# Weights stored by partition in the inputs of an eight-core retention and mixture-of-experts layer

## The chip, the cores and the metric

The kernel runs on the eight cores of one Trainium2 chip. Each core takes one of the eight sequences of the input (2048 tokens of width 1024) and holds its own copy of all weights; the cores exchange nothing. The metric is device time in microseconds of the slowest core.

## What is computed

One layer in two halves. Everything is given in float32; the kernel multiplies in bfloat16.

```python
x = x + attn(layernorm(x))        # retention, 16 heads of 64
x = x + ffn(layernorm(x))         # 8 experts, 2 per token, and a shared part

# attn: q, k, v per head; scores = (q k^T) * decay; ret = scores v; norm per head
gate = x @ w1                     # 1024 x 1024
out = (silu(gate) + norm) @ w2    # 1024 x 1024

# ffn
probs = softmax(x @ router_w); top 2 of 8 experts
routed = sum over the two of p_e * (silu(x @ w1[e]) @ w2[e])       # 8 x 2 matrices of 1024 x 1024
shared = sigmoid(x @ shared_gate_w) * ((silu(g) * u) @ shared_down) # g, u = halves of x @ shared_gate_up (1024 x 2048)
```

## The kernel before, in words

The weights lie in the inputs as the reference has them, row by row in float32. TensorE wants them in bfloat16 with row k * 128 + p in partition p. DMAs issued by GpSimd (POOL) convert the type on the way, and so all weights pass through the queue that the profile calls q0:

- `cast_rows` (L327) loads a matrix straight into SBUF: `w1a` (L328, the gate), `rout` (the router, nine columns), `w2a`, `wgu` and `wdn` (the shared part). Each partition reads eight rows of the matrix, one for each k, that lie 128 rows apart.
- `cast_step` (L901) converts the experts' matrices from HBM to a bfloat16 copy `wbd` in HBM, in 64 DMAs of 256 source rows each. Each writes two rows of 2 KB side by side in each of 128 partitions.
- `ew_ready` (L974) later loads the converted matrices of an expert into one of four SBUF buffers `ew`, with two DMAs of 2 MB on SP's queue (q1). An expert's partition has 32 KB in `wbd`, and each DMA takes one 16 KB half of it.

The first stage handles the 2048 tokens in eight groups of two tiles (128 tokens each). A program in Python lays the steps of retention, projection, router and shared part of neighbouring groups over one another by due times (the table AT) and emits them in that order to every engine. POOL's order is fixed by it too: it computes the reciprocal roots of the layer norms (L369) and of the head norms (L585), issues the casts of the experts, about nine to a group (L906), and the scatters of the routing table (L820, `metad`). Tiles of x are loaded by SP (`load_x`, L305): tile t + 2 is asked for at the statistics of tile t, tiles 4 and later wait for the first small products since they share their space, and tile t waits for the output of tile t - 10.

SP's order at the start is: x0, wk, x1, four constants, x2, x3, six constants, a block of zeros (`zrow`), the table's padding (`padm`), x4 to x7. ACT issues wq, eye and wv on its own queue (q10). POOL issues `w1a` at once; `rout`, `w2a`, `wgu`, `wdn` come in its program behind the roots of tiles x0 and x1, and the first experts' casts behind those of x4 and x5 (L369).

At the end of the first stage the last four scatters write which token goes where (L820). SP reads the table back (`meta`, L1001), POOL gathers the first expert's tokens with it (L1033), and TensorE transposes them (L1045). Then come the eight experts, first layer L1062, second layer L1106 (L1082 for the last half block), and each block's result is added to the output by an indirect DMA (L1117, L1091). An extra branch for experts with over 576 tokens isn't taken here.

Of the kernel before, what the change touches and what calls it, by code (L numbers as in the profile page):

```python
# [8 lines left out]
BF16 = mybir.dt.bfloat16  # L9
# [5 lines left out]
D = 1024  # L15
T = 2048
NH = 16
NE = 8
# [124 lines left out]
def build():  # L143
    nc = bass.Bass("TRN2", target_bir_lowering=False)
    st = contextlib.ExitStack()

    def din(name, shape, dt=F32):
        return nc.dram_tensor(name, shape, dt, kind="ExternalInput").ap()
# [2 lines left out]
    dwq = din("wqT", [128, NH * 64])  # L151
    dwk = din("wkT", [128, NH * 32])
    dwv = din("wvb", [128, 1024])
    dw1a = din("w1a", [D, D])
    dw2a = din("w2a", [D, D])
    dgns = din("gns", [128, 8])
    dgnb = din("gnb", [128, 8])
    drout = din("rout", [D, 9])
    dwe1 = din("we1", [NE, D, D])
    dwe2 = din("we2", [NE, D, D])  # L160
    dwgu = din("wgu", [D, 2 * D])
    dwdn = din("wdn", [D, D])
    deye = din("eye", [128, 128], BF16)
    dtri = din("tri", [128, 128], BF16)
    dstri = din("stri", [128, 128], BF16)
# [6 lines left out]
    dout = nc.dram_tensor("out", [T + PAD, D], F32, kind="ExternalOutput").ap()  # L172

    dx2r = nc.dram_tensor("x2rd", [T + PAD, D], BF16).ap()
    dwb = nc.dram_tensor("wbd", [NE, 128, 16384], BF16).ap()
    dmeta = nc.dram_tensor("metad", [128 * NSB, 2], I32).ap()
    NPL = EB * NE + 4 * OVC * NE

# [43 lines left out]
    rout = al("rout_sb", [128, 72], BF16)  # L222
# [3 lines left out]
    w1a = al("w1a_sb", [128, 8192], BF16)  # L226
# [14 lines left out]
    w2a = al("w2a_sb", [128, 8192], BF16)  # L241
# [8 lines left out]
    wgu = al("wgu_sb", [128, 16384], BF16)  # L250
    wdn = al("wdn_sb", [128, 8192], BF16)
# [12 lines left out]
    ew = [al(f"ew{i}", [128, 16384], BF16, a) for i, a in enumerate((Z1, Z2, Z3, Z3 + 32768))]  # L264
# [18 lines left out]
    p = Prog(nc, st)  # L283
# [19 lines left out]
    K = {}  # L303
# [21 lines left out]
                       (ones, dones))  # L325

    def cast_rows(dst, src):  # L327
        return lambda e: e.dma_start(out=dst[:, :].rearrange("p (k f) -> p k f", k=8),  # L328
                                     in_=src.rearrange("(k p) f -> p k f", p=128))
    k_w1a = p.dma("gpsimd", s_w["w1a"], cast_rows(w1a, dw1a[:, :]))  # L330

    k_z = [p.op("vector", lambda e, i=i: e.memset(sbd[i][:, :], 0.0)) for i in range(2)]
# [568 lines left out]
    def cast_step(e_, w_, q):  # L901
        src = (dwe1, dwe2)[w_]

        def f():
            a = 8192 * w_ + 2048 * q
            k_cast[e_] = p.dma("gpsimd", s_cast[e_], lambda e: e.dma_start(  # L906
                out=dwb[e_, :, a:a + 2048].rearrange("p (k f) -> p k f", k=2),
                in_=src[e_, 256 * q:256 * q + 256, :].rearrange("(k p) f -> p k f", p=128)))
        return f
    casts = [cast_step(e_, w_, q) for e_ in range(NE) for w_ in range(2) for q in range(4)]  # L910

# [1 line left out]
    for f in (a0, b0, score_weights, c0, a1, b1, c1_, center):  # L913
# [5 lines left out]
        out=dx2r[T:T + PAD, :].rearrange("(b p) f -> p b f", p=128),  # L919
        in_=zrow[:, :].unsqueeze(1).broadcast_to([128, PAD // 128, D])), k_pre0)  # L920
# [53 lines left out]
    def ew_ready(e_, *ws):  # L974
        for w_ in range(2):
            k_ew[e_, w_] = p.dma("sync", s_ew[2 * e_ + w_], lambda e, w_=w_: e.dma_start(
                out=ew[e_ % 4][:, 8192 * w_:8192 * w_ + 8192], in_=dwb[e_, :, 8192 * w_:8192 * w_ + 8192]),
                k_cast[e_], *ws)
    ew_ready(0, end_1)


# [17 lines left out]
    for f in sct7:  # L999
        f()  # L1000
    k_meta = p.dma("sync", s_meta, lambda e: e.dma_start(  # L1001
        out=meta[:, :].rearrange("p (b c) -> p b c", c=2), in_=metad[:, 0:EB * NE, :]), K["sct"])
    k_meta4 = None
    for h in range(2):
        k_meta4 = p.dma("sync", s_meta4, lambda e, h=h: e.dma_start(
            out=meta4[64 * h:64 * h + 64, :].rearrange("p (b c) -> p b c", c=2),
            in_=metad[0:64, 0:EB * NE, :]), K["sct"], end_1)
# [3 lines left out]
    k = p.op("vector", lambda e: e.tensor_reduce(flag[:, :], carry[:, :], AXX, ALU.max), vecf)  # L1011
# [138 lines left out]
    for eng in ("tensor", "vector", "scalar"):  # L1150
# [4 lines left out]
        out=ovm[:, :].rearrange("p (b c) -> p b c", c=2), in_=metad[:, EB * NE:NPL, :]), k_acc)  # L1155
    ovf = ovm[:, :].bitcast(F32)
    last = None
    for e_ in range(NE):
        for w_, src in enumerate((dwe1, dwe2)):
            kw = p.dma("gpsimd", s_ovw, lambda e, e_=e_, w_=w_, src=src: e.dma_start(  # L1160
                out=ew[0][:, 8192 * w_:8192 * w_ + 8192].rearrange("p (k f) -> p k f", k=8),
                in_=src[e_, :, :].rearrange("(k p) f -> p k f", p=128)), last, K["L2", NE - 1])
        for c in range(OVC):
            n0 = 4 * (OVC * e_ + c)
            kf = []
            for i in range(4):
                n = n0 + i
                kx = p.dma("gpsimd", s_xs[i], lambda e, n=n, i=i: e.indirect_dma_start(
                    out=xs[i][:, :], out_offset=None, in_=dx2r[:, :],
                    in_offset=bass.IndirectOffsetOnAxis(ap=ovm[:, 2 * n:2 * n + 1], axis=0)), last, k_om)  # L1170
                kb, bank, w = rot.take()
                bv = as_bf(bank)

                def fl(e, i=i, bv=bv):
                    for q in range(8):
                        m = e.transpose(bv[:, 128 * q:128 * q + 128], xs[i][:, 128 * q:128 * q + 128],
                                        eye[:, :])
                    return m
                k = p.op("tensor", fl, kx, w)
                kf.append(p.op("vector", lambda e, i=i, bv=bv: e.tensor_copy(  # L1180
                    xst[0][:, 0:4096].rearrange("p (k s) -> p k s", k=8)[:, :, 128 * i:128 * i + 128],
                    bv.rearrange("p (k s) -> p k s", k=8)), k, K.get("ovl1")))
                rot.done(kb, kf[-1])
            kh = []
            for f_ in range(8):
                kb, bank, w = rot.take()

                def f1(e, f_=f_, bank=bank):
                    for q in range(8):
                        m = e.matmul(bank[:, :], ew[0][:, 1024 * q + 128 * f_:1024 * q + 128 * f_ + 128],  # L1190
                                     xst[0][:, 512 * q:512 * q + 512], start=(q == 0), stop=(q == 7))
                    return m
                K["ovl1"] = k = p.op("tensor", f1, kf, kw, w)
                kh.append(p.op("scalar", lambda e, f_=f_, bank=bank: e.activation(
                    hT[0][:, 512 * f_:512 * f_ + 512], bank[:, :], AF.Silu), k, K.get("ovl2")))
                rot.done(kb, kh[-1])
            done = []
            for i in range(4):
                n = n0 + i
                ky = []  # L1200
                for h in range(2):
                    kb, bank, w = rot.take()

                    def f2(e, i=i, h=h, bank=bank):
                        for q in range(8):
                            m = e.matmul(bank[:, :], hT[0][:, 512 * q + 128 * i:512 * q + 128 * i + 128],
                                         ew[0][:, 8192 + 1024 * q + 512 * h:8192 + 1024 * q + 512 * h + 512],
                                         start=(q == 0), stop=(q == 7))
                        return m
                    K["ovl2"] = k = p.op("tensor", f2, kh, w)  # L1210
                    ky.append(p.op("scalar", lambda e, i=i, h=h, n=n, bank=bank: e.mul(
                        yb[i][:, 512 * h:512 * h + 512], bank[:, :], ovf[:, 2 * n + 1:2 * n + 2]), k,
                        k_acc, last, k_om))
                    rot.done(kb, ky[-1])
                done.append(p.dma("gpsimd", s_acc[i], lambda e, i=i, n=n: e.indirect_dma_start(
                    out=dout[:, :], out_offset=bass.IndirectOffsetOnAxis(ap=ovm[:, 2 * n:2 * n + 1], axis=0),
                    in_=yb[i][:, :], in_offset=None, compute_op=ALU.add), ky, done))
            last = [done, K["ovl1"], K["ovl2"]]
# [21 lines left out]
def _host_prep(inputs):  # L1240
    gam = _gammas()
    bf = lambda x: np.ascontiguousarray(x).astype(ml_dtypes.bfloat16)
    f32 = lambda x: np.ascontiguousarray(x, dtype=np.float32)
# [18 lines left out]
    p = np.arange(128)  # L1262
    vtab = np.zeros((128, NT, NH))
    for t in range(NT):
# [6 lines left out]
    rcon[:, 0:16] = np.tile(8.0 - e8, 2)[None, :]  # L1271
    rcon[:, 16:32] = np.tile(128 * EB * e8, 2)[None, :]
    rcon[:, 32:48] = np.tile(128 * EB * NE - CAP + (512 * OVC - 128 * EB) * e8, 2)[None, :]
    rout = np.concatenate([np.asarray(inputs["L0_ffn_router_w"]),
                           np.asarray(inputs["L0_ffn_shared_gate_w"])], axis=1)
    return {
        "wqT": f32(wqT.reshape(128, -1)), "wkT": f32(wkT.reshape(128, -1)),
        "wvb": f32(wvb.reshape(128, -1)),
        "w1a": f32(inputs["L0_attn_w1"]), "w2a": f32(inputs["L0_attn_w2"]),
        "gns": f32(np.asarray(inputs["L0_attn_gn_scale"]).reshape(8, 128).T),  # L1280
        "gnb": f32(np.asarray(inputs["L0_attn_gn_bias"]).reshape(8, 128).T),
        "rout": f32(rout),
        "we1": f32(inputs["L0_ffn_w1"]), "we2": f32(inputs["L0_ffn_w2"]),
        "wgu": f32(inputs["L0_ffn_shared_gate_up"]), "wdn": f32(inputs["L0_ffn_shared_down"]),
        "eye": bf(np.eye(128)), "tri": bf(tri), "stri": bf(stri), "ones": bf(np.ones((128, 128))),
        "sel": bf(sel), "selb": bf(selb.reshape(16, -1)),
        "vtab": f32(vtab.reshape(128, -1)), "etab": f32(etab.reshape(128, -1)),
# [17 lines left out]
```

How the kernel before makes its waits and increments, by code:

```python
        def go(e):  # L85
            for sem, value in need:
                e.wait_ge(sem, value)
            return fn(e)
# [2 lines left out]
    def op(self, eng, fn, *ws):  # L91
        sem = self.eng_sem[eng]
        self.count[eng] += 1
        self.raw(eng, lambda e: fn(e).then_inc(sem, 1), *ws)
        return Tok(sem, self.count[eng])
# [4 lines left out]
    def dma(self, eng, sem, fn, *ws):  # L100
        total = self.dma_total.get(sem.name, 0) + 16
        self.dma_total[sem.name] = total
        self.raw(eng, lambda e: fn(e).then_inc(sem, 16), *ws)
        return Tok(sem, total)
```

## Time and profile before

| | us |
|---|---|
| median of 3 runs | 814.59 (810.98 to 815.88) |
| the profiled execution | 814.13 |
| its span, slowest core | 812.6 (cores from 807.7 to 812.6) |
| first stage, to TensorE's last product before the routed tokens | 479.4 |
| TensorE begins on the experts | 517.4 |

The span is what lies between a core's first and last instruction; the profiled execution's time is 1.5 us longer. All numbers of the trace are of core 7, the slowest, unless a core is named. Its DMA queues are q0 (POOL), q1 (SP) and q10 (ACT). A DMA is cut into packets, and the 16 DMA engines take a share of the packets each; the profile gives bytes as they are written, so that a float32 matrix that arrives as bfloat16 counts half of what is read.

### The profile page before, as it was taken

The page shows a single profiled execution, that of the slowest core. Times are in us where ns is not written, and L with a number is a line of the kernel's source. Part 1 is how long each engine was busy: PE and PEld are TensorE (multiplying, and loading weights), DVE is VectorE, ACT ScalarE, POOL GpSimd, SP SyncE. Part 2 cuts the span into 40 slices and gives each one's busy share as a digit, 9 for nine tenths or more (in the row PEclk, how much of TensorE's full clock was granted, in tenths as well). Part 3 has the DMA queues.
Part 4 walks back from the last instruction along what each step waited for, and adds up shares of the span by engine and source line. Part 5 has one row for each costly group of instructions (what it writes and reads, how often), then busy time and mean ns, then how long its engine had stood idle before and what let it go on. Part 6 is the DMA issues. An engine that isn't in the chain of part 4 may idle for free.

```text
span 812.6 us, 15482 instructions; the slowest of 8 cores (807.7 to 812.6 us)
## 1 busy us (share of the span) xinstructions
PE 676.5 (83%) x5736; PEld 453.4 (56%) x5736; DVE 322.9 (40%) x872; ACT 282.6 (35%) x482; POOL 247.0 (30%) x241
## 2 busy tenths in 40 slices
PE   2478799797997997988987850499999999999990
PEld 2354585574764855756665630376575765756650
DVE  4446577486584773854857620110010100101000
ACT  2363633434426334343142100033333343333430
POOL 1242504414226044133240300424344243440321
PEclk9978999899898998998999985599999999999996
DMA  9999999999999999999999994869999998992843
GB/s 193 218 206 153 180 134 114 149 150 111 126 149 138 135 131 134 111 110 149 108 128 250 146 235 50 262 227 171 242 231 199 266 208 219 237 218 41 117 57 64
DMA packets 44640, 131.30 MB, mean 162 GB/s; under 512 B 7040, under 2 KB 7424, under 8 KB 42512
## 3 DMA queue, kind: packets, MB, share of 16 engines
q0 software_dynamic: 32336, 72.41, 67.3%
q1 hardware_dynamic: 11792, 56.75, 24.9%
q10 hardware_dynamic: 432, 1.08, 0.5%
q8 instruction: 49, 0.80, 0.4%
q14 instruction: 31, 0.25, 0.1%
HBM read 141.35 MB, written 66.49 MB: 256 GB/s over the span
## 4 chain that ended last, share of the span: by engine, by line
PE 66%; DVE 11%; DMA 9%; issue 5%; POOL 3%; ACT 2%; another core or an unknown queue 1%; SPq 1%; DVEq 0%; POOLq 0%; ACTq 0%
PE P L1062 16%; PE P L1106 14%; PE P L843 13%; DMA metad<-ext,pos 5%; PE P L458 4%; PE P L654 4%; DMA xr<-x 3%; DVE stt L364 3%; PE P L868 2%; PE P L1045 2%; POOL rstd L585 2%; DVE pb L507 2%; PE P L1082 2%; PE P L442 1%; PE P L416 1%
## 5 line engine op out<-in xcount | busy, mean ns | idle before, releaser
L1062 PE MATMUL P<-xst,ew 128*128 128x288 bf16 x1024 | 134.9, 289 | 1.1 <-DVE xst L1049 1.1
L843 PE MATMUL P<-x2T,wgu_sb 128*128 128x256 bf16 x1024 | 129.7, 291 | 0.5 <-DVE xr L879 0.5
L843 PEld LDWEIGHTS P<-x2T,wgu_sb 128*128 128x128 bf16 x1024 | 105.8, 105 | 20.1 <-issue 1.0
L1062 PEld LDWEIGHTS P<-xst,ew 128*128 128x128 bf16 x1024 | 98.6, 99 | 28.7 <-issue 4.2
L1106 PE MATMUL P<-ew,hT 128*128 128x512 bf16 x512 | 111.8, 379 | 0.0
L1049 DVE COPY xst<-P 128x1024 bf16<-128x1024 bf16 (+1 forms) x40 | 25.5, 638 | 209.3 <-PE P L1045 209.3
L1069 ACT ACTIVATE hT<-P 128x288 bf16<-128x288 f32 x128 | 52.7, 412 | 141.5 <-PE P L1062 81.9
L585 POOL TENSOR_TENSOR rstd<-gtmp,mhalf 128x16 bf16<-128x16 f32 x16 | 46.7, 2918 | 175.4 <-DVE gtmp L581 175.4
L1117 POOL DMA_INDIRECT out<-yb,meta x32 | 50.4, 1575 | 107.9 <-ACT yb L1112 84.0
L1106 PEld LDWEIGHTS P<-ew,hT 128*128 128x128 bf16 x512 | 50.0, 98 | 58.9
L1033 POOL DMA_INDIRECT xs<-x2rd,meta x40 | 38.1, 952 | 117.0 <-PE P L1045 63.0
L1112 ACT ACTIVATE yb<-P,meta 128x512 f32<-128x512 f32 x64 | 44.1, 689 | 69.1 <-PE P L1106 65.9
L654 PE MATMUL P<-w2a_sb,gate 128*128 128x512 bf16 x256 | 61.3, 384 | 5.9 <-DVE gtmp L581 3.3
L868 PE MATMUL P<-wdn_sb,sgu 128*128 128x512 bf16 x256 | 60.5, 379 | 5.1 <-issue 4.1
L458 PE MATMUL P<-xnt,w1a_sb 128*128 128x256 bf16 x512 | 64.2, 281 | 0.0
L1045 PE MATMUL P<-eye_sb,xs 128*128 128x128 bf16 (+1 forms) x320 | 24.2, 222 | 38.6 <-DMA xs<-x2rd,meta 38.6
L458 PEld LDWEIGHTS P<-xnt,w1a_sb 128*128 128x128 bf16 x512 | 49.5, 100 | 11.0 <-issue 2.1
L369 POOL TENSOR_TENSOR mv<-mv,mhalf 128x1 f32<-128x1 f32 x32 | 17.8, 555 | 114.1 <-DVE mv L368 111.0
L672 ACT ACTIVATE x<-xr,mv 128x1024 bf16<-128x1024 f32 x16 | 19.9, 1244 | 81.4 <-DVE mv L374 81.2
L364 DVE BATCH_NORM_STATS2 stt<-xr 128x6 f32<-128x512 f32 x64 | 41.0, 683 | 13.0 <-DMA xr<-x 12.7
L906 POOL DMA_DIRECT2D wbd<-we x64 | 45.3, 720 | 0.0
L1045 PEld LDWEIGHTS P<-eye_sb,xs 128*128 128x128 bf16 (+1 forms) x320 | 20.5, 101 | 42.8 <-issue 41.2
(134 smaller groups left out, 834.2 us busy)
## 6 DMA issues: line engine op xcount, KB each, us to landing
wbd<-we POOLq DMA_DIRECT2D x64, 512.0 KB
ew<-wbd SPq DMA_DIRECT2D x16, 2048.0 KB, 23.3
xr<-x SPq DMA_DIRECT2D x16, 512.0 KB, 16.4
out<-xr SPq DMA_DIRECT2D x16, 512.0 KB, 17.5
wgu_sb<-wgu POOLq DMA_DIRECT2D x1, 4096.0 KB, 61.4
x2rd<-x SPq DMA_DIRECT2D x16, 256.0 KB
w1a_sb<-w1a POOLq DMA_DIRECT2D x1, 2048.0 KB, 29.2
w2a_sb<-w2a POOLq DMA_DIRECT2D x1, 2048.0 KB, 35.3
```

Source lines behind the costliest of these rows:

```text
L364: a = [p.op("vector", lambda e, h=h: e.bn_stats(sv[:, 6 * h:6 * h + 6], src[:, 512 * h:512 * h + 512]), k_src, K.get(("mvfree", i))) for h ...
L458: last = e.matmul(bank[:, GT * j:GT * j + GT], w1a[:, 1024 * k + 128 * mm:1024 * k + 128 * mm + 128], xv[:, GT * k:GT * k + GT], start=(k ...
L585: K["rs", t] = p.op("gpsimd", lambda e: e.tensor_tensor(rstd[:, 32 * par + 16 * i:32 * par + 16 * i + 16], gtmp[:, 16 * i:16 * i + 16], mh ...
L654: last = e.matmul(bank[:, :], gate[par][:, GT * k + 128 * i:GT * k + 128 * i + 128], w2a[:, 1024 * k + 512 * h:1024 * k + 512 * h + 512], ...
L843: last = e.matmul(bank[:, GT * j:GT * j + GT], wgu[:, 2048 * k + a:2048 * k + a + 128], x2T[b][:, GT * k:GT * k + GT], start=(k == 0), sto ...
L868: last = e.matmul(bank[:, :], sgu[:, GT * k + 128 * i:GT * k + 128 * i + 128], wdn[:, 1024 * k + 512 * h:1024 * k + 512 * h + 512], start= ...
L906: k_cast[e_] = p.dma("gpsimd", s_cast[e_], lambda e: e.dma_start(out=dwb[e_, :, a:a + 2048].rearrange("p (k f) -> p k f", k=2), in_=src[e_ ...
L1045: last = e.transpose(bv[:, n * k:n * k + n], xs[i][0:n, 128 * k:128 * k + 128], eye[0:n, 0:n])
L1062: last = e.matmul(bank[:, 0:HC], ew[e_ % 4][:, 1024 * k + 128 * f_:1024 * k + 128 * f_ + 128], xst[e_ % 2][:, CAP * k + HC * c:CAP * k + H ...
L1069: K["h", e_, c] = p.op("scalar", lambda e: e.activation(hT[e_ % 2][:, CAP * f_ + HC * c:CAP * f_ + HC * c + HC], bank[:, 0:HC], AF.Silu), ...
L1106: last = e.matmul(bank[:, :], hT[e_ % 2][:, CAP * k + 128 * i:CAP * k + 128 * i + 128], ew[e_ % 4][:, 8192 + 1024 * k + 512 * h:8192 + 102 ...
L1117: K["acc", n] = p.dma("gpsimd", s_acc[n % 4], lambda e: e.indirect_dma_start(out=dout[:, :], out_offset=bass.IndirectOffsetOnAxis(ap=meta[ ...
```

## The change

Each weight matrix comes in as 128 rows, one for each partition, with the eight pieces of the partition side by side. The function `rows` on the host makes that order. Loads and casts then take whole rows: 32 KB of float32 that become 16 KB of bfloat16 (64 KB and 32 KB for `wgu`, 288 bytes for the router). A cast of an expert's matrix, of which there are still four to a matrix, now takes 32 whole partitions, every fourth one, and each matrix of `wbd` is one contiguous block of 2 MB. The number of DMAs, their order, their waits and their bytes are as before.

```diff
-    dw1a = din("w1a", [D, D])
-    dw2a = din("w2a", [D, D])
+    dw1a = din("w1a", [128, 8192])
+    dw2a = din("w2a", [128, 8192])
-    drout = din("rout", [D, 9])
-    dwe1 = din("we1", [NE, D, D])
-    dwe2 = din("we2", [NE, D, D])
-    dwgu = din("wgu", [D, 2 * D])
-    dwdn = din("wdn", [D, D])
+    drout = din("rout", [128, 72])
+    dwe1 = din("we1", [NE, 128, 8192])
+    dwe2 = din("we2", [NE, 128, 8192])
+    dwgu = din("wgu", [128, 16384])
+    dwdn = din("wdn", [128, 8192])
-    dwb = nc.dram_tensor("wbd", [NE, 128, 16384], BF16).ap()
+    dwb = nc.dram_tensor("wbd", [NE, 2, 128, 8192], BF16).ap()
     def cast_rows(dst, src):
-        return lambda e: e.dma_start(out=dst[:, :].rearrange("p (k f) -> p k f", k=8),
-                                     in_=src.rearrange("(k p) f -> p k f", p=128))
+        return lambda e: e.dma_start(out=dst[:, :], in_=src)
...
         def f():
-            a = 8192 * w_ + 2048 * q
             k_cast[e_] = p.dma("gpsimd", s_cast[e_], lambda e: e.dma_start(
-                out=dwb[e_, :, a:a + 2048].rearrange("p (k f) -> p k f", k=2),
-                in_=src[e_, 256 * q:256 * q + 256, :].rearrange("(k p) f -> p k f", p=128)))
+                out=dwb[e_, w_, q:128:4, :], in_=src[e_, q:128:4, :]))
...
             k_ew[e_, w_] = p.dma("sync", s_ew[2 * e_ + w_], lambda e, w_=w_: e.dma_start(
-                out=ew[e_ % 4][:, 8192 * w_:8192 * w_ + 8192], in_=dwb[e_, :, 8192 * w_:8192 * w_ + 8192]),
+                out=ew[e_ % 4][:, 8192 * w_:8192 * w_ + 8192], in_=dwb[e_, w_, :, :]),
                 k_cast[e_], *ws)
...
+    rows = lambda w: f32(np.asarray(w).reshape(*np.shape(w)[:-2], 8, 128, -1).swapaxes(-3, -2).reshape(
+        *np.shape(w)[:-2], 128, -1))
```

## Rows read from the trace of the kernel before

**Rows 1.** The page: busy shares, the span in 40 slices, POOL's queue.

```profile
PE 676.5 (83%) x5736; PEld 453.4 (56%) x5736; DVE 322.9 (40%) x872; ACT 282.6 (35%) x482; POOL 247.0 (30%) x241
PEclk9978999899898998998999985599999999999996
DMA  9999999999999999999999994869999998992843
GB/s 193 218 206 153 180 134 114 149 150 111 126 149 138 135 131 134 111 110 149 108 128 250 146 235 50 262 227 171 242 231 199 266 208 219 237 218 41 117 57 64
...
q0 software_dynamic: 32336, 72.41, 67.3%
```

**Rows 2.** The timeline of TensorE from 472 us: start, length, line [idle before, releaser].

```profile
472.35 7.07 PE L868 MATMUL P<-wdn_sb,sgu 128*128 128x512 bf16 x32 [1.01 <-DVE sgu L854]
517.41 1.01 PE L1045 MATMUL P<-eye_sb,xs 128*128 128x128 bf16 x8 [37.99 <-DMA xs<-x2rd,meta]
```

**Rows 3.** The chain that ended last, in order of time: start, length, what.

```profile
466.07 40.08 DMA metad<-ext,pos
506.22 1.88 DMA meta<-metad
...
509.26 1.00 POOL xs L1033
510.53 8.25 DMA xs<-x2rd,meta
```

**Rows 4.** The same chain of core 4.

```profile
456.92 45.26 DMA metad<-ext,pos
```

**Rows 5.** The stretches of one group and one expert: busy us by engine, PEclk, DMA share, GB/s.

```profile
205.00:260.00 55.00, 50.25 (x471) 34.49 (x470) 35.87 (x102) 22.82 (x38) 18.76 (x21) 0.93 1.05 140
...
658.00:692.00 34.00, 34.00 (x252) 21.67 (x252) 3.19 (x5) 12.80 (x25) 12.65 (x10) 1.00 0.92 221
```

**Rows 6.** DMA queues, 18 to 24 us: packets, MB, share of 16 engines.

```profile
q0 software_dynamic: 382, 0.78, 80.2%
q1 hardware_dynamic: 387, 0.51, 29.3%
```

**Rows 7.** DMA queues, 42 to 48 us.

```profile
q0 software_dynamic: 226, 0.46, 58.7%
q1 hardware_dynamic: 227, 0.80, 43.2%
```

**Rows 8.** DMA queues, 60 to 70 us.

```profile
q0 software_dynamic: 350, 1.43, 99.0%
```

**Rows 9.** DMA queues, 120 to 135 us.

```profile
q0 software_dynamic: 844, 1.63, 99.9%
```

**Rows 10.** DMA queues, 471 to 476 us.

```profile
q1 hardware_dynamic: 80, 1.23, 79.0%
q0 software_dynamic: 89, 0.16, 22.9%
```

**Rows 11.** DMA queue of SP, 0 to 60 us, and 24 to 30 us.

```profile
q1 hardware_dynamic: 3424, 6.33, 37.7%
...
q1 hardware_dynamic: 768, 0.81, 52.1%
```

**Rows 12.** The timeline of POOL: start, length, line [idle before, releaser].

```profile
16.95 0.55 POOL L369 TENSOR_TENSOR mv<-mv,mhalf 128x1 f32<-128x1 f32 x1 [5.85 <-DVE mv L368]
...
23.14 0.89 POOL L328 DMA_DIRECT2D w2a_sb<-w2a  x1
...
57.20 0.55 POOL L369 TENSOR_TENSOR mv<-mv,mhalf 128x1 f32<-128x1 f32 x1
57.70 4.16 POOL L906 DMA_DIRECT2D wbd<-we  x6
...
466.07 0.96 POOL L820 DMA_INDIRECT metad<-ext,pos  x1 [0.27 <-issue]
```

**Rows 13.** Who waited for x: us in total, times, longest; SP's issue; x loads' landing.

```profile
DVE stt L364 <- DMA xr<-x: 12.7, 4, 4.1
...
28.14 2.17 SPq L306 DMA_DIRECT2D xr<-x  x4
...
xr<-x SPq DMA_DIRECT2D x16, 512.0 KB, 16.4
```

More of the change, by code:

```diff
@@ L1160, in build @@
             kw = p.dma("gpsimd", s_ovw, lambda e, e_=e_, w_=w_, src=src: e.dma_start(
-                out=ew[0][:, 8192 * w_:8192 * w_ + 8192].rearrange("p (k f) -> p k f", k=8),
-                in_=src[e_, :, :].rearrange("(k p) f -> p k f", p=128)), last, K["L2", NE - 1])
+                out=ew[0][:, 8192 * w_:8192 * w_ + 8192], in_=src[e_, :, :]), last, K["L2", NE - 1])
         for c in range(OVC):
@@ L1278, in _host_prep @@
         "wvb": f32(wvb.reshape(128, -1)),
-        "w1a": f32(inputs["L0_attn_w1"]), "w2a": f32(inputs["L0_attn_w2"]),
+        "w1a": rows(inputs["L0_attn_w1"]), "w2a": rows(inputs["L0_attn_w2"]),
         "gns": f32(np.asarray(inputs["L0_attn_gn_scale"]).reshape(8, 128).T),
         "gnb": f32(np.asarray(inputs["L0_attn_gn_bias"]).reshape(8, 128).T),
-        "rout": f32(rout),
-        "we1": f32(inputs["L0_ffn_w1"]), "we2": f32(inputs["L0_ffn_w2"]),
-        "wgu": f32(inputs["L0_ffn_shared_gate_up"]), "wdn": f32(inputs["L0_ffn_shared_down"]),
+        "rout": rows(rout),
+        "we1": rows(inputs["L0_ffn_w1"]), "we2": rows(inputs["L0_ffn_w2"]),
+        "wgu": rows(inputs["L0_ffn_shared_gate_up"]), "wdn": rows(inputs["L0_ffn_shared_down"]),
         "eye": bf(np.eye(128)), "tri": bf(tri), "stri": bf(stri), "ones": bf(np.ones((128, 128))),
```

## The prediction

> **What bounds the kernel now.** First the page. TensorE is busy for 83% of the span, but the DMA engines stand at nine tenths from the second slice to the twenty-fifth, while they write only 110 to 150 GB/s over most of it [rows 1]. The stretches show two regimes [rows 5]. In a group of the first stage (55 us) TensorE works for 50 us and the DMA share is above 1; in an expert (34 us) TensorE is busy for the whole 34.0 us, and DMAs there cost nothing. So the question is the first stage.
>
> TensorE's timeline shows one hole: its last product of the first stage ends at 479.42, the next begins at 517.41, 38 us later, and what ends the wait is the gather of the first tokens [rows 2]. The chain says what the gather waited for [rows 3]: the last scatter of the routing table, issued at 466.07 on POOL, takes 40.08 us to land, for 8 bytes a row. The table's load (1.88 us), POOL and the gather (8.25 us) follow. The scatter is a small thing at the end of a long queue: casts go through q0 too, and they were behind. Core 4 tells the same: its scatter left 9 us earlier, at 456.92, and landed at 502.2, hardly earlier [rows 4]. The end of the first stage is set by when the DMA engines are through with their work, not by when the scatter is asked for.
>
> **The price of a cast.** A packet's time is the share times 16 engines times the stretch, over the packets. Into SBUF, 2 KB written (4 KB read) takes 0.802 x 96 / 382 = 0.201 us [rows 6]; `wgu`, with runs twice as long, 0.990 x 160 / 350 = 0.453 us for 4 KB written, or 0.226 us for 2 KB [rows 8]. So a run of double length was no cheaper by the byte. From HBM to HBM, a 2 KB packet takes 0.999 x 240 / 844 = 0.284 us [rows 9]. The trace has no HBM to HBM packet over 2 KB, so what the change makes of 0.284 us isn't shown. Its bounds are 0.201 us (only the destination's place costs, the nearest row below) and 0.32 us for 2 KB (0.284 worsened as `wgu` is against rows 6, by 12%). A cast moves three bytes through HBM for each it writes: 1.63 MB in 15 us is 326 GB/s of HBM traffic, and the `wgu` load's 1.43 MB in 10 us is 286 GB/s of reading. Both are of the size of the best stretches, in which large loads of plain type land 1.23 MB in 5 us, 246 GB/s, beside casts of 0.16 MB (another 96 GB/s through HBM) [rows 10]. That looks like memory with eight cores on it, not like a cost by the packet, and I take 0.284 us as it is: no gain from longer runs.
>
> The Trainium skill, HBM Reference, Specifications, gives about 358 GB/s for each core of a pair; by that figure the cast-only stretch has 9% left at most, an estimate of some 26 us over the 291 us that all casts cost. It also puts the size needed for line rate at 512 bytes (DMA: Bandwidth & Descriptors, Specifications), and by that rule the runs were long enough before; the rows agree between 2 and 4 KB.
>
> **What a turn is.** An engine takes packets from its queues in turns. From 42 to 48 us q0 moved 226 packets and q1 227 [rows 7], from 18 to 24 us 382 and 387 [rows 6]. From 471 to 476 us q1's packets are 16 KB rows of `ew` (1.23 MB in 80), q0's 2 KB, and it is still 89 to 80 [rows 10]: one for one whatever the size, and q1 has 79% of the engines' time then. So whoever has the longer rows gets the engine. The change gives q0 rows of 16 KB, with 8 x 0.226 = 1.8 us each into SBUF and 8 x 0.284 = 2.3 us in HBM. That each row stays one packet is a reading: q1's 16 KB rows are one each, and `wgu`'s 4 KB too (350 packets, 1.43 MB). The other end is that q0's packets stay at 4 KB, the longest that this queue shows.
>
> The Trainium skill has the turns too (DMA: Bandwidth & Descriptors, Queues, rings and completion order): an engine goes round its queues and drains one packet, typically 9 to 17 descriptors, from each. Were q0's turn already nine 2 KB rows, it would last 2.6 us before as after, the start below would lose nothing, and the sum would stay near 814 us. The trace's one for one speaks against that reading.
>
> **The start.** This is where small packets of x now meet long ones of the weights. SP's order up to x7 is 3,424 packets by 60 us [rows 11], and x4 to x7 are the last 512 of them. Before x5 is complete, 3,168 must be through, 198 for each engine. x4 and x5 matter since POOL issues the first casts behind the root of x5 at 57.20 [rows 12], and TensorE's second group needs both tiles. Step by step with rows of 16 KB:
> - `w1a` starts at about 8.5 us as before. Its 8 rows for each engine take turns with one packet of q1 and one of q10 each, about 2.1 us a turn: done at 25 us. q1 is then near 384 packets, which is x0, wk and x1. x1 is at hand at about 26 us rather than before the root at 16.95.
> - `w2a` is 6.2 us behind that root in POOL's program [rows 12]. It leaves at about 34 us and moves at 38. In between q1 is almost alone: at 768 packets in 6 us [rows 11] it would finish, but SP issues `zrow`, `padm` and x4 to x7 (28.14 before [rows 13]) also some 10 us later. I put q1 at 2,300 of 3,168 by 38 us, so 54 are left for each engine. x2 and x3 come by 36 us rather than 30, six lost.
> - Now `w2a`, `wgu` and `wdn`: 256 pieces of 2 KB for each engine, between 0.201 and 0.226 us, so 51 to 58 us; I take 55. They are 24 rows (32 if `wgu`'s are cut in two), and q1 gets 24 packets in between (5 us); the other 30 cost 6 us. x5 is there at 38 + 55 + 5 + 6 = 104 us instead of 57: **+47 us**, and TensorE and POOL stand still for it. If q0's packets stay at 4 KB, a turn is 0.2 us longer over some 50 turns: +10 us. The upper end is +55.
>
> **The later groups.** Nine casts a group are 146 pieces for each engine, 42 us, and q1's 48 packets (two loads, two outputs, two `x2rd`) another 10: 52 of 54.5 us. The order shifts, the work fits. But a load of x waits for an output to land, and both now take turns of 2.3 + 0.2 us against a median of 16.4 us to landing [rows 13]: eight packets are 20 us. Today only the first four tiles are waited for, 12.7 us in total [rows 13]. I take +4 us for three such loads, from 0 to 12.
>
> **The hand-over.** What TensorE loses at the start, the casts make up: they wait for x5 themselves, so the loads of the weights are through before the first is issued, and the backlog of about 42 us that stood through the first stage isn't built. So the last scatter, at 466.07 + 47, doesn't wait 40.08 us. It still has 16 rows of `ew` for each engine beside it (0.790 x 80 / 80 = 0.79 us each [rows 10], 13 us at most); bounds are 3 us and 13 us, I take 6. That is **-34 us**. The clock comes back after that hole in any case (two slices at 0.5 [rows 1]); it now has a hole at the start too, for about 1 us.
>
> **At nothing.** `rout` becomes 128 packets rather than 1,024, some 4 us of q0 that the start's sum already holds. Issues on POOL cost about 0.7 us a cast [rows 12] with idle time around. The contiguous `ew` loads lie beside TensorE in the experts; without that cover they would decide, but 34.0 of 34 us are TensorE's [rows 5].
>
> **Sum**, against the profiled execution's 814.13 us (its span and 1.5 us around it, and 0.5 us under the median of 814.59): 814.13 + 47 + 4 - 34 + 1 = **832 us**.
>
> **Rivals.**
> 1. *The casts do get cheaper and the turns don't hurt* (cheaper runs in HBM, or an engine that cuts long rows so that x passes). For it: 0.284 against 0.201 us for the same 2 KB is a difference of place that may be one of runs. Against it: `wgu`. From 0.25 us downwards the 1,024 pieces for each engine are 35 us less and the backlog is gone. Then the scatter takes 3 us, and the rest of the chain (3.1 us to POOL's gather, 8.2 to TensorE) ends at 467 + 3 + 11.3 = 481 us, just behind TensorE's own end. That is 36 us gained, about 5 lost to the loads of `ew`: **784 us**, between 775 and 800.
> 2. *Nothing but the router's load changes*: packets are cut to the old size, or to 4 KB with +10 us at the start that the queue's end gives back. The work of the engines is what it was, less 4 us: **811 us**, 805 to 818.
> 3. *Slower, and further than I say*: SP's queue starves in every group. The place is the six casts that POOL issues in a row at the start of a group: 12 rows of 2.3 us for each engine. An output and the load that waits for it can then take 20 us each, one behind the other, and the load is asked for about 22 us before its tile is due. From a landing of about 25 us on, each of four groups loses 10 us or more: **860 us**.
>
> **How the numbers follow.** Forecast 0.50, rival 1 0.27, rival 2 0.15, rival 3 0.08. The forecast's own range is 816 (lower ends of start and groups) to 848 (both upper ends and the scatter at 13). The range for all must reach into rival 1: 782 to 848 leaves out rival 3 and the fastest part of rival 1, under 0.2. A measurement here tells no change from one within about 1%, 806.4 to 822.7 us. Slower is four fifths of the forecast and rival 3, 0.48; the rest of the forecast and most of rival 2 is the same, 0.22; rival 1 and a little of rival 2 is faster, 0.30.
>
> **What would show it.** q0's packets fall from 32,336 [rows 1] to about half (the gathers, scatters and results stay), and rows of 16 KB appear; if they don't, rival 2 holds or the weaker start. x5's root stands near 100 us, with TensorE idle before it for over 30 us: the start. The last scatter lands in under 13 us: the hand-over. TensorE's group keeps about 55 us, or rival 3. The price of 2 KB in a cast-only stretch stays near 0.284 us, or rival 1. I am wrong if long rows don't hold an engine for their whole length, and wrong by the other sign if they do but cost much less.

## The result, and the profile after

| | before | after |
|---|---|---|
| median, us | 814.69 (810.98 to 815.88, 4 runs) | 835.08 (832.13 to 835.27, 4 runs) |
| span of the profiled execution, slowest core | 812.6 | 833.6 |
| spans of all its cores | 807.7 to 812.6 | 805.3 to 833.6 |

The ratio is 1.0249, between 1.0216 and 1.0283: 20 us slower, where 832 us had been forecast. After the change core 4 is the slowest, and the rows of after are core 4's. Its own span before was 810.0 us. Some executions run slower, with the cores of one die at a lower clock: all ratios leave them out, the medians in us hold every run, and E2's profiled execution is read on its other die, cores 4 to 7.

The page of after, with the share of the DMA engines in 40 slices and the two large queues (packets, MB, share of 16 engines over the span):

```profile
span 833.6 us, 15437 instructions; the slowest of 8 cores (805.3 to 833.6 us)
PE 676.8 (81%) x5691; PEld 455.1 (55%) x5736; DVE 322.9 (39%) x872; ACT 281.0 (34%) x482; POOL 233.6 (28%) x241
DMA  8899999999999999989797947797999999992743
q0 software_dynamic: 13520, 72.41, 61.2%
q1 hardware_dynamic: 11792, 56.75, 25.7%
```

TensorE has the same work as in [rows 1]. POOL's queue carries the same 72.41 MB in 13,520 packets instead of 32,336, and its share fell: 0.612 x 833.6 = 510 us of the engines' time, where core 7 had 0.673 x 812.6 = 547 us before. Compared core by core, the DMA engines had 21 to 38 us less to do (34 us on core 4; 27 us on core 0, from 67.8% of 810.5 to 64.5% of 809.9), and the kernel is 20 us slower all the same. The slices say how: inside the first stage, slices 18, 20, 22 and 24 stand at 8, 7, 7 and 4 where [rows 1] have 9. The engines wait in the middle of the stage that they used to bound.

**The turns.** DMA queues of after, each a stretch named here: 40 to 50 us (rows of `w2a`, 16 KB as written), then 60 to 80 us (rows of `wgu`, 32 KB), then 130 to 140 us (casts beside x):

```profile
q0 software_dynamic: 83, 1.36, 99.9%
q1 hardware_dynamic: 84, 0.27, 8.7%
...
q0 software_dynamic: 102, 3.34, 95.6%
q1 hardware_dynamic: 102, 0.39, 6.9%
...
q0 software_dynamic: 98, 1.08, 98.5%
q1 hardware_dynamic: 95, 0.16, 4.7%
```

In [rows 6, 7] the two queues shared packet for packet with 2 KB rows; they still do, with rows of 16 and 32 KB, each of them one packet (3.34 MB in 102). SP's queue gets 8.7% and 6.9% of the engines in these stretches, where it had 43.2% and 29.3% in those of [rows 7, 6]. The Trainium skill (DMA: Bandwidth & Descriptors, Queues, rings and completion order) lets a turn hold 9 to 17 descriptors; these counts show turns of one row, whatever its length.

**The start.** POOL's timeline (start, length, line): the root of x1, the issue of `w2a`, the root of x5 with the first casts behind it, the last cast, the last scatter:

```profile
27.04 0.55 POOL L368 TENSOR_TENSOR mv<-mv,mhalf 128x1 f32<-128x1 f32 x1 [16.30 <-DVE mv L367]
33.23 0.55 POOL L328 DMA_DIRECT2D w2a_sb<-w2a  x1
87.48 0.55 POOL L368 TENSOR_TENSOR mv<-mv,mhalf 128x1 f32<-128x1 f32 x1 [20.59 <-DVE mv L373]
87.98 3.04 POOL L904 DMA_DIRECT2D wbd<-we  x6
465.51 0.57 POOL L904 DMA_DIRECT2D wbd<-we  x1
519.40 0.96 POOL L819 DMA_INDIRECT metad<-ext,pos  x1 [0.31 <-issue]
```

The same on core 4 before: first casts 57.08, last cast 408.76, last scatter 456.92. So the first casts are 30.9 us late, the last one 56.8, the scatter 62.5.

**The middle.** Who waited for x (us in total, times, longest), and from the chain that ended last, in order of time (start, length, what):

```profile
DVE stt L363 <- DMA xr<-x: 73.3, 7, 22.0
```

```profile
33.53 27.78 DMA xr<-x
...
206.18 38.88 DMA out<-xr
245.13 5.58 DMA xr<-x
...
293.25 20.18 DMA out<-xr
...
354.23 8.25 DMA xr<-x
...
519.40 8.35 DMA metad<-ext,pos
527.82 1.99 DMA meta<-metad
...
532.26 7.09 DMA xs<-x2rd,meta
```

Before it was 12.7 us of waiting, all of it in the first four tiles [rows 13]. Now there are seven waits of up to 22 us, and the chain names the cause of those in the middle: an output takes 38.9 us to land, and SP asks for the next tile of x only then, since both use one buffer. SP's own timeline shows it standing still between the two, and a load of x issued just ahead of the output:

```profile
205.76 0.33 SPq L306 DMA_DIRECT2D xr<-x  x1
206.18 0.38 SPq L883 DMA_DIRECT2D out<-xr  x1
245.13 0.33 SPq L306 DMA_DIRECT2D xr<-x  x1
```

The DMA queues between 206.2 and 245 us:

```profile
q0 software_dynamic: 367, 3.85, 90.9%
q1 hardware_dynamic: 288, 1.05, 10.2%
```

So 18 packets for each engine went through SP's queue in 39 us: eight rows of the load, eight of the output behind them, and two more. At 38.8 / 18 = 2.2 us a turn that is the whole 38.9 us. The pair of a load and an output 0.4 us behind it comes again at 313.49 and 313.91 us, and SP's next load leaves at 354.23. The output of 293.25 is no comparison for it: only 1.56 MB of q0's went beside it, and it landed in 20.18 us.

**The hand-over.** The last scatter lands in 8.35 us instead of 40.08 and 45.26 us [rows 3, 4]. TensorE's first work on the experts:

```profile
536.65 0.99 PE L1042 MATMUL P<-eye_sb,xs 128*128 128x128 bf16 x8 [3.44 <-issue]
```

That is 17.25 us behind the scatter's issue, where core 4 had 55.6 us before (456.92 to 512.50). From there to the end it is 297.0 us, and was 297.5.

### The profile page after: what moved, and what is told of

Its sections match the earlier page's. It is cut to its first block, busy times and chain, and to the rows that moved or that the text cites. A ratio compares the mean times of both kernels' runs of the same rounds, so it can differ in the third digit from the quotient of the medians.

```text
span 833.6 us, 15437 instructions; the slowest of 8 cores (805.3 to 833.6 us)
## 1 busy us (share of the span) xinstructions
PE 676.8 (81%) x5691; PEld 455.1 (55%) x5736; DVE 322.9 (39%) x872; ACT 281.0 (34%) x482; POOL 233.6 (28%) x241
## 3 DMA queue, kind: packets, MB, share of 16 engines
q0 software_dynamic: 13520, 72.41, 61.2%
## 4 chain that ended last, share of the span: by engine, by line
PE 51%; DMA 17%; DVE 12%; issue 10%; another core or an unknown queue 3%; POOL 2%; ACT 2%; DVEq 1%; SPq 0%; ACTq 0%; POOLq 0%
PE P L1059 15%; PE P L1103 13%; PE P L842 8%; DMA xr<-x 8%; DMA out<-xr 7%; PE P L653 3%; DVE stt L363 2%; PE P L457 2%; PE P L1042 2%; DVE u L638 2%; PE P L1079 2%; DVE gate L642 2%; DVE pb L506 1%; POOL rstd L584 1%
## 5 line engine op out<-in xcount | busy, mean ns | idle before, releaser
L842 PE MATMUL P<-x2T,wgu_sb 128*128 128x256 bf16 x1024 | 132.2, 294 | 1.1 <-issue 0.6
L1103 PE MATMUL P<-ew,hT 128*128 128x512 bf16 x496 | 109.7, 379 | 0.9 <-ACT hT L1066 0.2
L867 PE MATMUL P<-wdn_sb,sgu 128*128 128x512 bf16 x237 | 57.5, 379 | 2.8 <-DVE sgu L853 1.2
L404 ACT ACTIVATE xn<-xr,mv 128x1024 bf16<-128x1024 f32 x16 | 19.8, 1237 | 77.4 <-DVE mv L373 77.4
L653 PEld LDWEIGHTS P<-w2a_sb,gate 128*128 128x128 bf16 x256 | 23.9, 100 | 33.6 <-issue 10.3
L506 DVE TENSOR_TENSOR pb<-P,tri_sb 128x512 bf16<-128x512 f32 x64 | 41.0, 683 | 2.7 <-PE P L497 2.4
## 6 DMA issues: line engine op xcount, KB each, us to landing
out<-xr SPq DMA_DIRECT2D x16, 512.0 KB, 10.3
```

The lines of the kernel that those rows point to most:

```text
L506: kk.append(p.op("vector", lambda e, n=n, b=b: e.tensor_tensor(dst[:, 512 * n:512 * n + 512].rearrange("p (s f) -> p s f", s=4), b[:, :].r ...
L653: last = e.matmul(bank[:, :], gate[par][:, GT * k + 128 * i:GT * k + 128 * i + 128], w2a[:, 1024 * k + 512 * h:1024 * k + 512 * h + 512], ...
L842: last = e.matmul(bank[:, GT * j:GT * j + GT], wgu[:, 2048 * k + a:2048 * k + a + 128], x2T[b][:, GT * k:GT * k + GT], start=(k == 0), sto ...
L867: last = e.matmul(bank[:, :], sgu[:, GT * k + 128 * i:GT * k + 128 * i + 128], wdn[:, 1024 * k + 512 * h:1024 * k + 512 * h + 512], start= ...
L1103: last = e.matmul(bank[:, :], hT[e_ % 2][:, CAP * k + 128 * i:CAP * k + 128 * i + 128], ew[e_ % 4][:, 8192 + 1024 * k + 512 * h:8192 + 102 ...
```

## The experiments

The experiments used three chips, and the kernel before ran at 815.88, 829.5 and 828.87 us on them; so times are compared on one chip only, and each ratio is to the kernel before on its chip. "x5's root", "the last scatter" and the like are medians over the eight cores of a profiled execution, from POOL's timeline: 55.5 and 455.5 us before, 87.2 and 509.9 us after.

### Which rows: all short, or the loads' or the casts' long

The first four keep the changed kernel's layout, with the router's load long, and cut its rows by 64 floats of padding behind each piece. E1 cuts everything to the old length, E2 only the casts, E3 only the loads, E4 everything to 2,048 elements. The core of E1, beside the changed kernel:

```diff
-    dwe1 = din("we1", [NE, 128, 8192])
+    dwe1 = din("we1", [NE, 128, 8704])
...
+    def cut(src, n):
...
+        return src.rearrange("p (k g) -> p k g", g=n + 64)[:, :, 0:n]
...
-                out=dwb[e_, w_, q:128:4, :], in_=src[e_, q:128:4, :]))
+                out=fit(dwb[e_, w_, q:128:4, :], 1024), in_=cut(src[e_, q:128:4, :], 1024)))
```

> The changed kernel with its new layout in memory, but each row cut into the old pieces: 4 KB read and 2 KB written (8 KB and 4 KB for wgu), by 256 bytes of padding between pieces in the inputs. Only the router's load stays long. Theory of turns (long packets on POOL's queue hold each engine and starve SP's queue): the loss is gone, x5's root is back near 57 us, the last scatter again waits about 40 us, 808 to 815 us against 814.6 before and 835 after. Rival, layout (the places and strides in HBM cost, not the packets): still 830 to 838 us. If short pieces with long contiguous reads are cheaper in memory: under 805 us.

> Long rows only for w1a, w2a, wgu, wdn and the router; the experts' casts are cut to 2 KB written. Theory of turns: the start keeps its loss (x5's root near 87 us rather than 57), the groups then go without a wait for x, and with the backlog gone the last scatter lands in under 10 us: 30 lost and about 32 given back, 810 to 819 us. Rival, layout: 825 us or more if the loads' layout costs, 814 with x5's root near 57 us if it doesn't. If the loss sat in the casts alone: the start at 57 us.

> Long rows only for the experts' casts (16 KB written, 2.3 us of an engine each); the loads of w1a, w2a, wgu, wdn are cut to the old pieces. Theory of turns: x5's root stays near 57 us, then SP's queue starves in the groups: waits for x of 20 us and more after outputs that take 30 us and more to land, 35 to 60 us up to the last scatter, and 30 of them given back at the hand-over: 820 to 840 us. Rival, only the start matters: x5's root at 57 us and no later waits, 805 to 815 us.

> All weights in pieces of 8 KB read and 4 KB written. Theory of turns: a turn of q0 is 0.45 to 0.57 us, x5's root 5 to 12 us later than 57, hardly a wait for x in the groups, the scatter's wait shorter by what the start lost, 808 to 816 us. Also the missing row, a cast of 4 KB from HBM to HBM: 0.57 us a packet if it goes by bytes; 0.45 us or less would be a gain from longer runs and give 795 us or less.

| | us | ratio | x5's root | waits for x | last scatter |
|---|---|---|---|---|---|
| E1, all short | 824.14 | 1.0082 [1.0051, 1.0114] | 70.8 | 30.7 | 468.0 |
| E2, loads long | 827.58 | 1.0112 [1.0060, 1.0164] | 86.7 | 46.6 | 479.1 |
| E3, casts long | 827.10 | 1.0151 [1.0099, 1.0203] | 71.0 | 72.7 | 509.6 |
| E4, 4 KB pieces | 816.62 | 1.0014 [0.9982, 1.0046] | 84.8 | 44.8 | 483.7 |

The two halves of the change act where the prediction had them. Long loads set x5's root: 86.7 us in E2 and 87.2 in the changed kernel, 71 in E1 and E3. Long casts set the waits for x in the later groups. The totals of the table mix these with the start, so here are the waits behind 95 us alone, medians over the eight cores: 28 us in the changed kernel, 41 in E3, and none in E1, E2 and E4 or in the kernel before. The slowest core's waits in E3, of which 41.0 us lie behind 95 us:

```profile
DVE stt L372 <- DMA xr<-x: 71.8, 10, 14.3
```

Several expectations failed. With all rows short, but the router's long, x5 was still at 70.8 us and not near 57, and E1 wasn't back at the time of before; E6 and E12 take that up. In E2 the last scatter was to land in under 10 us, and on cores 4 and 7 it took 32.18 and 35.72 us: with short casts the engines' work still ends the stage, however late it starts. E4's x5 was to be 5 to 12 us later and came 29 us later, half of which the router explains (E1, E6). It has 45 us of waits for x, nearly all at the start, and a scatter that leaves 28 us later than before, and still no loss that can be measured: TensorE is at the experts at 512.6 us (median), where it was at 513.6 before. The shorter backlog behind the last scatter gives back all of it.

### The amount of work: eight casts fewer

E5 is the kernel before without the casts of the second matrices of experts 1 and 3, which use their neighbour's instead, so its result is another one.

```diff
+            if w_ == 1 and e_ in (1, 3):
+                return
```

> The kernel before without 8 of its 64 casts (the second matrices of experts 1 and 3 aren't converted; those experts use the second matrix of the expert before them), so 4 MB less written by casts, 36 us of each engine's time at 0.284 us for 2 KB. If the 38 to 50 us hole before the experts is the engines' backlog, it shrinks by about 33 us and the time is 778 to 788 us. If it is the scatter's own latency or an order of queues, it stays and so does 814 us.

794.20 us, 0.9562 [0.9534, 0.9590]: 36 us less for eight casts of 64, whose pieces are 128 for each engine. That is 36 us at the 0.284 us of [rows 9], but 40 us at the median price of before and 43 us at E5's own (below). So most of the work's price comes back, and the exact agreement with 0.284 us is chance. TensorE's timeline of E5 (core 0), its last product of the first stage and the first on the experts:

```profile
464.74 7.07 PE L868 MATMUL P<-wdn_sb,sgu 128*128 128x512 bf16 x32 [1.01 <-DVE sgu L854]
497.83 1.01 PE L1047 MATMUL P<-eye_sb,xs 128*128 128x128 bf16 x8 [26.02 <-DMA xs<-x2rd,meta]
```

There is still a hole of 26 us (8 to 30 us over the cores; 38 to 51 in the profile of the kernel before). So before the change the engines' work does bound the stage, and rival 1's 36 us for some 35 us less work was sound as a price.

### The router's small packets

E6 is the kernel before with the router's load alone in 128 packets.

```diff
-    drout = din("rout", [D, 9])
+    drout = din("rout", [128, 72])
...
-    k_rout = p.dma("gpsimd", s_w["rout"], cast_rows(rout, drout[:, :]))
+    k_rout = p.dma("gpsimd", s_w["rout"], lambda e: e.dma_start(out=rout[:, :], in_=drout[:, :]))
```

> The kernel before with nothing changed but the router's load: 128 packets of 288 bytes read rather than 1,024 of 36 bytes. In the first experiment (all old pieces, router long) x5's root came at 70 us, not 57. Theory: the router's many tiny packets on POOL's queue were cheap turns, in which SP's queue moved one packet each at the start; without them those packets pair with 2 KB pieces of w2a. Then x5's root is at 65 to 72 us here too, and the time 812 to 820 us. Rival: that delay came from the padded pieces or the new places; then x5's root stays at 57 us and the time is 809 to 815 us.

837.44 us, 1.0068 [1.0027, 1.0110], and x5's root at 72.6 us. DMA queues from 24 to 36 us, first E6 (core 3), then the kernel before (core 7):

```profile
q0 software_dynamic: 812, 1.35, 76.9%
q1 hardware_dynamic: 826, 0.90, 28.9%
```

```profile
q1 hardware_dynamic: 1448, 1.82, 59.9%
q0 software_dynamic: 1447, 0.82, 58.1%
```

One for one in both. But before, about 1,000 of q0's turns were the router's rows of 36 bytes, which took little of q0's time (its share is 58.1% with them and 76.9% without) and let 622 more packets of SP's queue through. A load that looks wasteful was what let x through. It also accounts for E1, whose other rows are all short: 1.0082 there, 1.0068 here, with intervals that overlap. Beside it the long loads (E2, 1.0112) and the long casts (E3, 1.0151) cost about 0.4% and 0.8%, the first no more than the intervals leave open, and all of it together 2.5%, somewhat more than the parts.

### x first, and outputs from another queue

E7 is the changed kernel with x4 to x7 asked for ahead of `zrow` and `padm`. E8 does that too, and stores the outputs from ACT's queue some steps later, so that SP never waits for them.

```diff
+    for t in range(4, 8):
+        load_x(t)
```

```diff
-                K["out", t] = p.dma("sync", s_out[t % NX], lambda e: e.dma_start(
+                def go(t=t, x=x):
+                    K["out", t] = p.dma("scalar", s_out[t % NX], lambda e: e.dma_start(
...
+                late.append(go)
```

> The changed kernel with x4 to x7 asked for ahead of the block of zeros and the table's padding on SP's queue. Theory of turns: x5's root returns to 50 to 60 us, so the start's 30 us are back; then the casts pile up behind the loads as before and SP's queue starves in the groups for longer: waits for x in the groups 50 us or more, last scatter at 500 us or later, 815 to 835 us. Rival, the start was all that was lost: 800 to 806 us.

> As the run with x4 to x7 ahead, and the output tiles of the first stage stored from ACT's queue a few steps later, so that outputs and loads of x no longer stand behind one another in one queue and each queue has its own turn. Theory of turns: the waits for x in the groups fall below 20 us in all, and the cheaper bytes of the long rows are then kept: 785 to 808 us. If the order within SP's queue is not what makes x late, it is like the run without it.

E7: 844.67 us, 1.0198 [1.0146, 1.0250]. x5's root is at 61.8 us, 25 us earlier than in the changed kernel, and the loss is nearly the same. The edit did a second thing, though: `zrow` and `padm` now stood behind x4 to x7 and came among the long rows. On core 4 `padm` took 105.9 us to land, and 8.8 us in the changed kernel:

```profile
metad<-padm SPq DMA_DIRECT2D x1, 136.0 KB, 105.9
```

```profile
ACT x2T L689 <- DMA metad<-padm: 47.4, 1, 47.4
```

In the program ACT's first copy of `x2T` waits for both (`K["gu", -2]`). ACT stood still for 42.8 to 48.5 us on all eight cores, and TensorE with it, 48.3 us on core 4. Behind that the chain of core 4 goes on:

```profile
192.74 13.91 DMA out<-xr
207.13 40.07 DMA out<-xr
247.27 18.16 DMA xr<-x
...
329.81 39.66 DMA out<-xr
369.56 14.60 DMA xr<-x
```

Outputs take 40 us here too (both were issued 0.4 us behind a load of x), SP waits for them, and the last scatter leaves at 520.6 us, no earlier than in the changed kernel. But the waits for x behind 95 us are 14 us (median), less than the changed kernel's 28. What used up the 25 us is first of all the wait for `padm`, which is longer than they are. So E7 doesn't show what an early x5 alone would bring, and it doesn't decide between its two expectations.

E8: four runs of 838.32, 844.25, 877.64 and 911.63 us, too far apart for a ratio; the lowest two are 1.1% and 1.8% over the kernel before. Its profiled execution, the fastest of them, has 26.8 us of waiting for x, of which 8 us behind 95 us, and still the last scatter at 517 us. It has the same wait for `padm`, 43.2 to 48.4 us over its cores, so what the other queue alone is worth stays open.

### Long rows where they can do least harm

E9 is the kernel before with long rows for the casts of experts 5 to 7 only, the last 24; E10 for those of experts 4 to 7; E11 is E9 with long loads of the weights and the router and x4 to x7 first. E12 has the changed kernel's layout of the experts' matrices and of `wbd`, but each cast takes every second partition and every second piece, so that its packets keep the old length.

```diff
+            if e_ >= LONG:
+                k_cast[e_] = p.dma("gpsimd", s_cast[e_], lambda e: e.dma_start(
+                    out=dwb[e_, q:128:4, 8192 * w_:8192 * w_ + 8192],
+                    in_=(dwl1, dwl2)[w_][e_ - LONG, q:128:4, :]))
+                return
```

```diff
+            def part(x):
+                return x[q % 2:128:2, :].rearrange("p (k c f) -> p k c f", c=2, f=1024)[:, :, q // 2, :]
...
+                out=part(dwb[e_, w_]), in_=part(src[e_])))
```

> The kernel before, with long rows only for the casts of experts 5 to 7, the last 24 of 64: they are issued after about 280 us, when nearly all tiles of x have been asked for, so that a starved SP queue can no longer make x late. If long rows cost an engine 0.293 us for 2 KB in such stretches rather than 0.322, 24 casts save 11 us of each engine's work, and as the first stage ends with that work the time is 6 to 13 us under before. If the turns still hurt there (x15, outputs, ew): no gain or a loss of up to 5 us.

> The same with experts 4 to 7, 32 casts, from about 245 us on: 15 us of work saved, but x13 to x15 are still to be asked for. Theory of turns: waits for x of 5 to 20 us come back in one or two groups, which the backlog covers in part: 5 to 15 us under before. If late tiles of x cost in full, slower than the run with three experts.

> The casts of experts 5 to 7 long, those of 0 to 4 as before, the loads of w1a, w2a, wgu, wdn and the router long, and x4 to x7 asked for ahead of the zeros and the padding. The start costs what the run with x4 to x7 ahead showed, x5's root at 62 us rather than 57; the loads' cheaper bytes and the router save 12 us of the engines' work and the late casts 11: 12 to 23 us under before. If the start's 5 us and the later x1 cost in full on top of an unchanged end: 0 to 8 us under.

> The kernel before with the experts' matrices and wbd laid out by partition as in the change, but each cast takes every second partition and every second piece, so that all packets stay at 4 KB read and 2 KB written, without padding; router and loads as before. The run with short padded pieces cost 0.342 us for 2 KB in cast-only stretches against 0.322 before. If the places cost that, it is 0.335 us or more here and the time 8 to 16 us over before; if it was the padding or the router, 0.322 us and no change within 4 us.

| | us | ratio | x5's root | waits for x | last scatter |
|---|---|---|---|---|---|
| E9, experts 5 to 7 | 827.50 | 0.9982 [0.9951, 1.0013] | 56.6 | 17.0 | 480.4 |
| E10, experts 4 to 7 | 829.79 | 1.0019 [0.9985, 1.0053] | 56.6 | 24.1 | 487.1 |
| E11, mixed | 831.95 | 1.0044 [1.0014, 1.0074] | 61.7 | 18.6 | 502.1 |
| E12, new places, short | 828.06 | 0.9987 [0.9952, 1.0021] | 56.4 | 13.6 | 454.9 |

E12's slowest core waits for x as the kernel before did:

```profile
DVE stt L364 <- DMA xr<-x: 13.7, 4, 4.7
```

E12 settles where the loss of the casts lies: with the experts' matrices laid out by partition and the packets short, nothing is lost and nothing gained. For the other weights E1 beside E6 says the same within their intervals. It is the length of the packets, not the places in memory. The price of E12's casts, which was to tell too, doesn't decide: as a mean over the stretches of the next section it is 0.340 us, the size expected if the places cost (0.322 before, 0.342 in E1), as a median 0.320 (0.315 and 0.322). E9 spared most loads of x, and the starving moved to what SP's queue carries at the stage's end. ACT waited for `x2rd` to land, 12.9 to 24.9 us over its eight cores, and not at all in E12. Core 5's wait, and its chain:

```profile
ACT x L675 <- DMA x2rd<-x: 24.9, 2, 18.2
```

```profile
463.67 42.57 DMA x2rd<-x
507.25 17.33 DMA meta<-metad
```

Its last scatter leaves 25 us later than E12's (medians). E10 and E11 didn't gain what was expected of them either; E11 takes E7's order over, and with it a wait for `padm` of 8.5 to 19.5 us. No version beat the kernel before.

### What a cast costs, over all kernels

From all 10 us stretches of cores 0, 2, 4 and 7 (4 to 7 in E2) between 110 and 470 us in which q1 has under 1.5% of the engines: q0's share of the 160 us, over its bytes in pieces of 2 KB, median, in us.

| chip | casts short | casts long |
|---|---|---|
| before and after, profiled | 0.315 | 0.297 |
| first (E1, E2; E3) | 0.322, 0.319 | 0.296 |
| second (E5, E6; E7, E8) | 0.336, 0.317 | 0.298, 0.301 |
| third (E12) | 0.320 | |

E4's pieces of twice the old length cost 0.315. Within each line long rows are 5 to 11% cheaper. At 0.297 us a core moves 16 x 3 x 2,048 bytes in that time, an estimate of 331 GB/s of HBM traffic. The Trainium skill (HBM Reference, Specifications) has 358 GB/s for a core; the runs stay under it, and long rows come nearer.

## Why the prediction was right, and where its terms were off

The time (832 against 835.08) and the mechanism hold; two terms were wrong, the start by 16 us and the groups by 28 us, with opposite signs. Core 4's own sum, from its rows above: +30.9 (start) + 25.8 (from the first cast to the last, 351.7 us before and 377.5 after) + 5.7 (last cast to last scatter, 48.2 and 53.9) - 38.3 (scatter to TensorE) - 0.5 (the rest) = 23.6 us, which is its 833.6 against 810.0.

- **What a turn is** held in full: one row for one row, at 16 and at 32 KB, and rows stay whole. q0's packets are less than half (13,520 of 32,336). Rival 2, that nothing but the router changes, falls with it.
- **The start: +47 predicted, 30.9 measured.** The steps up to `w2a` came as written (x1's root 27.04 against 26, `w2a` 33.23 against 34). The failing step is "I put q1 at 2,300 of 3,168 by 38 us". From 0 to 40 us it was:

```profile
q1 hardware_dynamic: 2827, 4.22, 38.9%
```

  So only 341 packets, 21 for each engine, were left, and they found their turns beside the loads. The 54 of the prediction had SP issuing `zrow`, `padm` and x4 to x7 some 10 us late; x4 to x7 left at 33.53 us against 28.14 [rows 13], and almost alone on the engines q1 went 500 packets further. From 24 to 36 us:

```profile
q1 hardware_dynamic: 2085, 2.44, 62.8%
...
q0 software_dynamic: 145, 0.02, 2.7%
```

  `wgu` was cheaper too: 0.956 x 320 us over 1,631 pieces (3.34 MB) is 0.188 us for 2 KB, against 0.226 us before [rows 8].
- **`rout` at nothing** was wrong in kind. It was costed by the 4 us of q0's engines that it frees; what it gave was turns. E6 shows 16 us at x5's root (72.6 against 56.7 in E5 on the same chip) and 0.7% of the time for this line alone. No run shows the 4 us. In the prediction's sum it is part of the start, which came out smaller all the same.
- **The groups: +4 predicted, 25.8 and 5.7 measured on core 4.** The step that failed is "I take +4 us for three such loads". The landing of an output was put at eight turns, 20 us. The one at 293.25 took as long, with fewer long rows beside it; the one at 206.18 took 38.9 us, and 40.07 and 39.66 stand on E7's chain. The turns were sized about right, 2.2 us by the stretch from 206.2 to 245 us against 2.5. What was left out is that the output stands behind the rows of the load of x that SP issues 0.4 us before it, 18 turns instead of eight. The waits for x behind 95 us came to 26 us on core 4. That is rival 3's place (an output, and the load that waits for it): where it has 10 us or more lost in each of four groups, core 4 lost 31 in all. The cores differ a lot in this (spans of 805.3 to 833.6 us; from first to last cast the medians are 350.8 and 374.3 us, 23.5 lost), and why it hits some more than others is open.
- **The hand-over: -34 predicted, -38.3 measured.** The reason given holds: the backlog isn't built when the casts wait, and the scatter lands in 8.35 us where 6 was taken.
- **No gain from longer runs** was wrong by 6%: 0.315 to 0.297 us in stretches of casts alone, 18 us of the engines' work over 1,024 pieces (21 to 38 us for all of q0, from the pages of the eight cores). The 0.284 us of [rows 9] came from a favourable stretch, and `wgu`'s, on which the choice leaned, compared 4 KB with 2 KB and nothing longer. It changed the end little, since the engines now stand idle in the middle; E9 to E11 try to take that gain without the loss and give 0.998 to 1.004. E5 shows what less work is worth where x keeps pace. So rival 1's saving was about half real (18 us of its 35), and its second condition, that the turns don't hurt, is what failed.

In the sum: 47 + 4 - 34 + 1 = 18 us predicted over the span, 23.6 measured on core 4. The closeness of the number is luck, as the start was 16 us too dear and the groups 28 too cheap. The mechanism isn't: one cause, the long row's turn, stands behind both terms, and E2 has the first without the second, E3 the second without the long loads. Whether an earlier x5 would shorten the time wasn't shown, since E7 brought a new wait with it. A small reading was off too: [rows 1] have the DMA engines at nine tenths in slices 1 to 24, not from the second to the twenty-fifth.

## What to carry to other kernels

Queues on shared DMA engines take turns by the packet, so the packet's length sets each queue's share: before making a bulk queue's rows longer, look at what the other queue carries, and price its turns (rows for each engine times the long row's time) against the slack of who waits for it. Tiny packets in a bulk queue are cheap turns for its neighbours, and removing them isn't free. Where the engines' work bounds a stage, fewer bytes are worth most of their time (8 casts, 36 of 40 to 43 us), while cheaper bytes that starve another queue only move the wait. And an order moved ahead puts others behind: E7 brought x5 forward by 25 us and held ACT up for over 42 us with what it had overtaken.

## What the runs showed that was not expected

- A row of 32 KB written (64 KB read, with a change of type) is one packet and holds its engine for 0.188 x 16 = 3 us.
- 1,024 rows of 36 bytes in POOL's queue were worth 16 us at x5's root (E6 against E5), since as many packets of SP's queue went through beside them.
- An output asked for 0.4 us behind a load of x had 18 packets for each engine to wait for, its own eight among them, and landed in 38.9 us. The median output landed sooner than before (10.3 us on core 4 against 18.1), the longest much later (38.9 against 22.2).
- The median price of the same short cast is 0.315 us in the profile of before and 0.317 to 0.336 us in E1, E2, E5, E6 and E12. Single stretches cost far more (0.504 us on core 0 of E1 from 310 us), which lifts the means to 0.322 us before and 0.342 in E1. No cause was found.
